# Reciprocal roots on ScalarE as exp(-0.5 ln v), from one table of functions

## The reference, cut to what matters

```python
def _ln_c(v, eps=1e-06):                       # v is (32, 64, 56, 56), normalised over the 64 channels
    m = mean(v, axis=1); s = var(v, axis=1)
    return (v - m) / sqrt(s + eps)

def conv_block(y):                             # y = _ln_c(x)
    z = conv3x3(sign(y + move1), sign(w3) * mean|w3|)
    z = rprelu(y + z * inv1 + b1)              # inv = gamma / sqrt(var + 1e-5) for each channel
    q = conv1x1(sign(z + move2), sign(w_pw) * mean|w_pw|)
    return rprelu(z + q * inv2 + b2)
x = x + conv_block(_ln_c(x))

t = tokens(x)                                  # 100352 tokens of 64 channels
y = (t - mean) / sqrt(var + 1e-5)              # over the 64 channels of a token
probs = softmax(y @ gate_w + gate_b)           # 8 experts
e = argmax(probs); kept = position among the tokens of e < 15680
t = t + kept * probs[e] * (relu(y @ w1[e] + b1[e]) @ w2[e] + b2[e])
return back_to_nchw(t)
```

## Time and profile before

| | us |
|---|---|
| three runs | 1861.76, 1861.85, 1863.74 |
| their median | 1861.85 |
| the profiled execution, its own time | 1857.47 |
| its span, first to last instruction | 1855.7 |

### The profile page before, as it was taken

How to read it: one execution, slowest core, us unless ns; L and a number is a source line. 1 busy time by engine, 2 the same in 40 slices (tenths; PEclk the granted TensorE clock), 3 DMA queues, 4 the chain that set the end, 5 groups by cost and what they waited for, 6 DMA issues and landing times.

```text
span 1855.7 us, 41100 instructions
## 1 busy us (share of the span) xinstructions
PE 1568.8 (85%) x10341; PEld 847.0 (46%) x10341; DVE 1474.4 (79%) x3641; ACT 1233.0 (66%) x4066; POOL 1048.2 (56%) x1052
## 2 busy tenths in 40 slices
PE   6998898888888988887612999998989898989894
PEld 1343444433443433344401555565656565656562
DVE  3588978888788888888840888887878797979795
ACT  4778877688787778866511777765656565656561
POOL 3115665766566766666773666654545455545452
PEclk9998988989999999997755999999999999999996
DMA  9446976866555965443425877878979888888895
GB/s 237 77 109 142 177 173 131 178 145 166 144 145 112 164 150 142 119 99 96 104 80 151 243 200 196 231 218 254 289 241 306 249 283 266 270 268 273 260 298 200
DMA packets 302238, 351.92 MB, mean 190 GB/s; under 512 B 48452, under 2 KB 252452, under 8 KB 295940
## 3 DMA queue, kind: packets, MB, share of 16 engines
q1 hardware_dynamic: 260644, 264.23, 54.6%
q0 software_dynamic: 41120, 85.81, 15.3%
q10 hardware_dynamic: 320, 0.33, 0.1%
HBM read 179.70 MB, written 180.01 MB: 194 GB/s over the span
## 4 chain that ended last, share of the span: by engine, by line
PE 45%; DVE 21%; issue 17%; ACT 6%; POOL 6%; DMA 3%; DVEq 1%; SPq 1%; POOLq 0%; ACTq 0%
PE bank L826 10%; PE bank L836 9%; PE bank L735 5%; PE bank L817 4%; POOL pairs_by_group L492 4%; PE bank L697 3%; PE bank L794 3%; PE bank L844 3%; PE bank L745 2%; DVE X L1294 2%; PE bank L768 2%; POOL X L486 2%; DMA pairs_by_group<-ROWS,idx 2%; ACT SQR L960 1%; DVE N L1314 1%
## 5 line engine op out<-in xcount | busy, mean ns | idle before, releaser
L492 POOL DMA_INDIRECT pairs_by_group<-ROWS,idx x400 | 433.4, 1084 | 119.5 <-issue 113.1
L524 POOL DMA_INDIRECT results_by_pair<-X,PAIRNO x310 | 303.2, 978 | 270.5 <-PE bank L817 207.5
L980 ACT ACTIVATE X<-bank,X 128x256 f32<-128x256 f32 x693 | 283.8, 471 | 105.6 <-PE bank L826 105.6
L826 PE MATMUL bank<-X 64*128 64x256 f32 x1848 | 269.4, 410 | 48.7 <-DVE X L1294 48.1
L486 POOL TENSOR_TENSOR X<-Z,X 128x448 f32 (+1 forms) x112 | 141.2, 1261 | 265.0 <-DVE Z L1271 247.1
L836 PE MATMUL bank<-X 128*64 128x256 f32 x1848 | 255.9, 399 | 1.2 <-DVE X L1294 1.2
L735 PE MATMUL bank<-S,WB 128*128 128x448 bf16 x1008 | 231.0, 378 | 0.0
L524 POOL DMA_INDIRECT results_by_pair<-S,PAIRNO x152 | 155.4, 1022 | 105.0 <-PE bank L817 77.3
L973 ACT ACTIVATE X<-bank 128x256 f32<-128x256 f32 x231 | 88.6, 383 | 189.3 <-PE bank L817 186.5
L826 PEld LDWEIGHTS bank<-X 64*128 64x128 f32 x1848 | 168.4, 191 | 99.7 <-issue 85.4
L817 PE MATMUL bank<-ident,X 128*64 128x128 f32 x1848 | 154.9, 289 | 58.6 <-DMA X<-weights_by_group 58.0
(11 more groups left out here) (213 smaller groups left out, 3031.3 us busy)
## 6 DMA issues: line engine op xcount, KB each, us to landing
X<-weights_by_group SPq DMA_DIRECT2D x231, 258.5 KB
X<-pairs_by_group SPq DMA_DIRECT2D x231, 134.0 KB
pairs_by_group<-PAD SPq DMA_DIRECT2D x15, 1742.0 KB
X<-in_x_dram SPq DMA_DIRECT2D x16, 1568.0 KB, 8.1
block_output<-X SPq DMA_DIRECT2D x112, 224.0 KB, 2.0
ROWS<-block_output SPq DMA_DIRECT2D x16, 1568.0 KB
Z<-results_by_pair SPq DMA_DIRECT2D x16, 1568.0 KB, 10.9
out_dram<-ROWS SPq DMA_DIRECT2D x16, 1568.0 KB
```

The costliest lines, as they stand in the source:

```text
L492: pool.indirect_dma_start(rows, bass.IndirectOffsetOnAxis(ap=idx[0:m, p.odd, k:k + 1], axis=0), ROWS[0:m, p.odd, k, :], None).then_inc(s_s ...
L524: pool.indirect_dma_start(done, bass.IndirectOffsetOnAxis(ap=PAIRNO[:, u, j:j + 1], axis=0), RES[u][:, j, :], None,).then_inc(s_back[u], 16)
L826: mm(hidden(q), WR[b, ring, q // 2 * P:(q // 2 + 1) * P], XT[b, ring % 2, :], start=True, stop=True).then_inc(s_h, 1)
L980: last = A(HB[:, ring % 2, q, :], hidden(q), ACT.Relu, bias=WR[:, ring, at:at + 1])
```

## The change

ScalarE loads one table ahead of everything else, one that holds logarithm and exponential. Each of the three reciprocal roots becomes two activations: the logarithm of the variance into a tile that is free at that time, and the exponential of -0.5 times it into the tile that held the root before. The second waits for the first by a new semaphore. The Newton steps behind them, the exponentials of L935 and all other engines stay as they were.

```diff
+        s_setln = sem("setup_logarithm")
+        s_ln1 = sem("variance_logarithm")
+        s_ln2 = sem("row_variance_logarithm")
...
-        B1P, CA, SG2, B2P, NB2P, CB, TS, TA, TBB = 10, 12, 13, 14, 15, 16, 18, 20, 22
+        B1P, CA, SG2, B2P, NB2P, CB, TS, TA, TBB, TL = 10, 12, 13, 14, 15, 16, 18, 20, 22, 24
...
         def _(act):
             A = nc.scalar.activation
+            act.preload_act_table_set("natural_log_exp_and_others")
             for h in range(2):
                 act.dma_start(W3[h * C:h * C + C, :], w3.rearrange("o i a b -> o (i a b)")).then_inc(s_w, 16)
...
                     if nor and c == 0:
                         act.wait_ge(s_v1, nor.n + 1)
-                        A(RA1[:, :], VAR1[:, :], ACT.Abs_reciprocal_sqrt).then_inc(s_sd1, 1)
+                        A(RB1[:, :], VAR1[:, :], ACT.Ln).then_inc(s_ln1, 1)
+                        wait_apart(act, s_ln1, nor.n + 1)
+                        A(RA1[:, :], RB1[:, :], ACT.Exp, scale=-0.5).then_inc(s_sd1, 1)
...
                             act.wait_ge(s_setstep, VAR_STEP)
-                            A(col(TS, 2), col(TA, 2), ACT.Abs_reciprocal_sqrt).then_inc(s_setsd, 1)
+                            A(col(TL, 2), col(TA, 2), ACT.Ln).then_inc(s_setln, 1)
+                            act.wait_ge(s_setln, 1)
+                            A(col(TS, 2), col(TL, 2), ACT.Exp, scale=-0.5).then_inc(s_setsd, 1)
...
                     if rou and c == 2:
                         act.wait_ge(s_rv, rou.n + 1)
-                        A(r0[:, :], var2[:, :], ACT.Abs_reciprocal_sqrt).then_inc(s_rs, 1)
+                        A(ra[:, :], var2[:, :], ACT.Ln).then_inc(s_ln2, 1)
+                        wait_apart(act, s_ln2, rou.n + 1)
+                        A(r0[:, :], ra[:, :], ACT.Exp, scale=-0.5).then_inc(s_rs, 1)
```

## The result

The change made the kernel slower: 1886.95 us (four runs, 1879.76 to 1904.31) against 1862.8 us (four runs). The ratio is 1.013, with an interval of 1.0092 to 1.0168. A second set of runs of the same kernel gave 1.0133 (1.0087 to 1.0179). The forecast was slower, with 1867.5 us in a range of 1853 to 1874; the time lies above it.

What follows compares the result with a forecast made beforehand. In the eight passes, PE and POOL's X were taken as level, so most of ten chain loads give nothing back. 0.1 + 2.6 + 1.5 - 1.0 - 3.0 + 5.5 = +5.7 us on 1861.85, about 1867.5 us; all cases 1853 to 1874.

Steps and rivals of the forecast that it cites:

- The load at the front, +0.1: Start of ScalarE's queue, ahead of four weight DMAs: the one load costs +0.1 us, bounds 0 and +1.28.
- The clock behind the second wait, +5.5: Second L764 of eight passes: PE waits for POOL's X, its clock may fall; 0 to +11 us, middle +5.5.
- L900, +2.6: Pixel variances' root: the second activation adds 4.8 us, vanished loads return 2.7, two places +0.5; bounds -2.7 and +4.5.
- The give-back: L900, four places at the start of ScalarE's loop turn: load gone less added step, 0.68 us each, -2.7 us.
- the idle time named issue: ScalarE's idle time before L900's load in four places, VAR long there; 0.68 us comes back at each.
- two of the ten late places: L900, ten places where RA waited for DVE's VAR: in two the readers came later, so only eight times 0.60 counted.
- L932, +1.5 and -1.0: Token variances' root: the longer step costs 0 to +2.9 us over eleven passes, middle +1.5; the last pass saves 1.0.
- The -1.0 of the last pass: L932 in the last pass: DVE no longer waits behind a load, -1.28 + 0.26 = -1.0 us.
- L935, -3.0: Exponentials: the load's removal saves 1.0 us in each of three passes with room; -3.0, range 0 to -3.8.
- The rival of a faster kernel, in which X moves with PE: POOL's X comes earlier too, eight passes keep their 1.0 us, no clock fall; -7.8 us, 1854.0 us; chance 0.20.
- the dearer load of 2.66 us: Rival: each load also has some 1380 ns of draining; another 1.38 us back at eight loads, -11, 1851 us; chance 0.04.
- eight falls at 1.4 us, the dearest case of the forecast: Second L764: the clock falls in all eight passes, 1.4 us lost each, +11 us, 5.5 above the forecast sum.

Runs made afterwards that it cites:

- warm_start: The changed kernel with four extra matmuls in PE's wait at about 29 us; 1.0112 of the kernel before, first 3x3 convolution at 52.4 us.
- no_loads: The kernel before with the exponentials replaced by a copy, so all table loads but two at the set-up are gone and nothing is added; 1.0084 of the kernel before.
- fill_no_loads: The kernel before with extra constant matmuls in PE's waits and the exponentials replaced by a copy, removing all loads but two; 0.9943 of the kernel before.
- fill_before: The kernel before with extra constant matmuls in PE's waits (four at the start, six at c = 1 to 6 each pass); 0.9937 of the kernel before.
- fill_step_var: The kernel before with the extra matmuls in PE's waits and a dependent copy after the root at L900 alone, loads kept; 0.9993 of the kernel before.
- after_again: The changed kernel run once more, nothing altered; 1.0133 of the kernel before, first 3x3 convolution at 63.8 us.

## Why the prediction was wrong

**The load at the front, +0.1:** right; the issues of the weights' transfers lie beside it. What the sum has no term for is that L900's second activation also lengthens PE's first wait, from 3.8 to 4.4 us, and that PE may come back from it at the lower clock for up to 34 us. In two of four executions with this start the first convolution was 11 to 16 us behind warm_start's.

**The clock behind the second wait, +5.5:** this step failed, by its size. The direction was right: in the pass at 440 there is the shorter idle time at the first row matmul (1.27), the new one at the second (2.16) and the clock at 0.5 behind it, and without loads, nothing added, this comes in eight passes running. What failed is the sentence that in 3.4 us of lower clock 1.4 us are lost, 11 us at most. The clock stays low for up to 10.4 us, and such a stretch costs 4.3. The loads' removal costs 16 us with the clock free (no_loads) and 1 us with it held (fill_no_loads), so some 15 us are the clock's. The place was half right: in the changed kernel three of nine passes have the new wait, and two of the four long stretches lie behind the first row matmul, where the prediction had them partly free.

The step took the length from one stretch of the kernel before. The same trace has a stretch three times as long behind the first row matmul of another pass, and an upper bound from it would have held three times as much:

```profile
287.65 0.54 PE L764 MATMUL bank<-biasrow,ones 65*128 65x432 bf16 x1 [3.19 <-ACT SQR L960]
```
```profile
286.90:297.10 10.20, 9.45 (x29) 4.35 (x29) 8.52 (x14) 6.51 (x29) 8.60 (x7) 0.50 0.53 136
```

**L900, +2.6:** mis-sized too. Eight places at 0.60 less four times 0.68 was the sum; the added step alone measures 8 to 10 us with the clock held, as much as all sixteen places at 0.60 would make (9.6, an estimate). The give-back was counted against it in vain: the idle time named issue did fall from 11.0 us to 2.7, but with the clock held all loads together give back nothing that the runs can tell. And two of the ten late places had been left out as covered; in fill_step_var DVE waits behind the root in 13 passes.

**L932, +1.5 and -1.0:** 0.2%, some 3 us, not told from nothing, and no contradiction to the forecast's 0 to 2.9. The -1.0 of the last pass was not looked at by itself. **L935, -3.0:** not seen; fill_no_loads is no faster than fill_before.

By their sizes: 15 (clock) + 10 (L900) + 3 (L932) = 28 us against the measured 24, each known to some 6 us; that the parts simply add up is assumed, and the start is not in the sum. So the sign was forecast for reasons that held, but the two largest costs, the clock's and L900's, were each put at about a third of what the runs show. The rival of a faster kernel, in which X moves with PE, did not come, and neither did the dearer load of 2.66 us of the Trainium skill (ScalarE: Activation LUTs, What ACT_TABLE_LOAD costs): with the clock held, 31 loads less are worth nothing within 6 us, and no run here shows a second part. The Trainium skill's rule that matmuls come back throttled after each wait (TensorE: Matmul & The Clock Gate, HAM oscillation), whose own case has longer waits, for transfers, is borne out in part: all eight waits named above in no_loads have the lower clock behind them, but after the wait of 1.70 us at 448.63 us in the changed kernel the clock is 1.00 from 448.6 to 456.6. And eight falls at 1.4 us, the dearest case of the forecast, would have been too little: one long stretch costs three times that.

**What stays open:** by which reader the second activation costs. VAR1's place and the order with the copy and the square were tried, and neither frees it; the Newton step's readers on DVE and POOL's blocks behind them are left, which no run isolates. Also why a stretch of the lower clock lasts 3.4 us in one pass and 10.4 in another, and why the start's slow stretch comes in some executions only.

## What to carry to other kernels

Time that an engine gains goes to the next wait of those that wait for it; find that wait first, and what TensorE's clock does behind it. Price a fall of the clock by the whole stretch that could follow at the new place, not by the stretch that follows at the old one. And to tell a cost of the clock from a cost of the path, run both kernels with a few matmuls of constants in PE's waits: here that split the loss in two halves, and made the kernel before 0.63% faster.

## What the runs showed of the hardware

After a wait of some four microseconds at the start, the same fp32 matmuls came back to the full clock after very different times. In the kernel before the granted clock was 0.50 from 34.4 to 37.8 us. In the changed kernel PE worked without a gap from 34.4 to 68.0 us at 0.50 throughout. In after_again it was without a gap too, at 0.50 from 34.0 to 58.6 and at 1.00 from 58.8 to 63.7, still on fp32 matmuls:

```profile
34.00:58.60 24.60, 24.60 (x29) 5.55 (x30) 3.71 (x6) 7.92 (x15) 0.00 (x0) 0.50 1.10 173
58.80:63.70 4.90, 4.90 (x12) 1.20 (x11) 1.86 (x3) 2.23 (x5) 0.00 (x0) 1.00 0.00 0
```

So a PE that is busy without a gap can stay at the lower level for over 30 us. The same instructions at the start gave first convolutions at 56.4, 57.2, 63.8 and 68.0 us in four executions.
